# Transformer block stack: residual stream kept tokens-on-partitions, softmax mask added by VectorE, maximum subtracted by GpSimd, P.V two slots later

## What is computed

```
for i in range(6):
    # attention: x @ Wqkv, 16 heads of 64; q and k normalised by head, rotated (rotary tables with scale)
    # windows of 32 queries, 64 keys; sim = 8 q.k, masked, softmax, times v
    x = attn_layer(shift_tokens(x), Wqkv[i], ...) + x            # ends in out @ Wo
    # layernorm over 128 channels, W1 to 2 x 341, a * gelu(gate), W2, with biases
    x = ffn_layer(shift_tokens(x), ln_g[i], ln_b[i], W1[i], b1[i], W2[i], b2[i]) + x
def shift_tokens(t):                                             # second half of the channels comes from the token before
    a, s = jnp.split(t, 2, -1)
    return jnp.concatenate([a, pad(s)[:, :-1]], -1)
```

## Time and profile before

| | us |
|---|---|
| median of three runs | 1746.93 (1746.7 to 1748.54) |
| the profiled execution, its own time | 1748.49 |
| its span, first to last instruction | 1746.7 |
| PE busy in the span | 1695.2 (97%) |
| VectorE (DVE) | 1391.6 (80%) |
| ScalarE (ACT) | 1232.3 (71%) |
| GpSimd (POOL) | 1129.3 (65%) |
| DMA queue of SyncE (q1) | 82512 packets, 116.84 MB, 27.8% of 16 engines |

### The profile page before, as it was taken

How to read it: one execution, slowest core, us unless ns; L and a number is a source line. 1 busy time by engine, 2 the same in 40 slices (tenths; PEclk the granted TensorE clock), 3 DMA queues, 4 the chain that set the end, 5 groups by cost and what they waited for, 6 DMA issues and landing times.

```text
span 1746.7 us, 72189 instructions
## 1 busy us (share of the span) xinstructions
PE 1695.2 (97%) x30558; PEld 1198.8 (69%) x30558; DVE 1391.6 (80%) x2607; ACT 1232.3 (71%) x2173; POOL 1129.3 (65%) x1066
## 2 busy tenths in 40 slices
PE   5889999999999999999999999999999999999996
PEld 2356777777777777777777777777777777777774
DVE  4688888888888888888888888888888888888762
ACT  2256777777777677777777777777777777777763
POOL 0477676667766766776676676667766666776640
PEclk9799999999999999999999999999999999999998
DMA  3133223323222332222323322322322332322222
GB/s 106 24 93 69 61 57 75 84 70 71 66 59 73 86 75 59 71 61 61 89 66 80 71 60 60 86 70 71 77 63 56 75 88 70 71 63 59 59 56 73
DMA packets 82830, 121.45 MB, mean 70 GB/s; under 512 B 25168, under 2 KB 28752, under 8 KB 82256
## 3 DMA queue, kind: packets, MB, share of 16 engines
q1 hardware_dynamic: 82512, 116.84, 27.8%
HBM read 20.28 MB, written 2.10 MB: 13 GB/s over the span
## 4 chain that ended last, share of the span: by engine, by line
PE 94%; DVE 3%; ACT 2%; issue 1%; DMA 0%; SPq 0%; POOL 0%; DVEq 0%; POOLq 0%; ACTq 0%
PE QKb L452 20%; PE O L543 12%; PE F L525 11%; PE S L452 9%; PE VTb L475 9%; PE S L501 9%; PE S L513 5%; PE F L598 4%; PE F L553 4%; PE F L599 3%; PE S L494 2%; PE F L568 2%; PE F L587 1%; DVE t L833 1%; PE F L560 1%
## 5 line engine op out<-in xcount | busy, mean ns | idle before, releaser
L833 DVE TENSOR_TENSOR t<-QKb,table 128x1024 f32<-128x1024 f32 x384 | 469.3, 1222 | 191.2 <-ACT sq L648 190.9
L977 POOL TENSOR_TENSOR t<-t 128x512 f32<-128x512 f32 x384 | 488.1, 1271 | 202.1 <-DVE t L833 201.1
L956 POOL TENSOR_TENSOR t<-t,rn 128x512 f32<-128x512 f32 x384 | 401.0, 1045 | 163.7 <-DVE rn L880 163.7
L648 ACT ACTIVATE sq<-QKb 128x512 f32<-128x512 f32 x384 | 229.3, 597 | 377.6 <-PE QKb L452 377.6
L452 PE MATMUL QKb<-wq_sb,x_sh 128*128 128x512 f32 x768 | 412.4, 619 | 11.2 <-DVE t L833 10.6
L475 PEld LDWEIGHTS VTb<-cst,t 128*128 128x128 f32 x1536 | 191.9, 141 | 200.2 <-issue 199.0
L842 DVE TENSOR_REDUCE ss<-sq 128x16 f32<-128x1024 f32 x192 | 232.0, 1208 | 0.0
L475 PE MATMUL VTb<-cst,t 128*128 128x128 f32 x1536 | 230.7, 273 | 0.0
L543 PEld LDWEIGHTS O<-PT,V 64*64 64x64 f32 x12288 | 196.7, 135 | 48.2 <-issue 42.4
L543 PE MATMUL O<-PT,V 64*64 64x32 f32 x12288 | 218.0, 221 | 0.4 <-DVE rn L880 0.4
L963 POOL TENSOR_TENSOR E<-E,rs 128x512 f32<-128x512 f32 x192 | 200.0, 1042 | 14.8 <-DVE rs L889 14.7
(11 more groups left out here) (137 smaller groups left out, 2464.2 us busy)
## 6 DMA issues: line engine op xcount, KB each, us to landing
V<-v_tok SPq DMA_DIRECT2D x1440, 64.0 KB, 2.0
wq_sb<-in_wqkv SPq DMA_DIRECT2D x36, 256.0 KB, 3.0
wo_sb<-in_wo SPq DMA_DIRECT2D x6, 512.0 KB, 4.3
w_sb<-in_w SPq DMA_DIRECT2D x6, 341.0 KB, 3.3
w_sb<-in_w SPq DMA_DIRECT2D x6, 192.0 KB, 3.0
y_spill<-OT SPq DMA_DIRECT2D x1, 1024.0 KB, 4.2
V<-y_spill SPq DMA_DIRECT2D x1, 1024.0 KB, 8.3
out<-V SPq DMA_DIRECT2D x4, 256.0 KB, 2.9
```

The costliest lines, as they stand in the source:

```text
L648: act.activation(sq[:, v % 4, :], QK_ps, ACT.Square).then_inc(sq_done, 1)
L833: dve.tensor_tensor(t12[:, v, :, :].rearrange("p c (h d) -> p c h d", h=8), QK_ps.rearrange("p (h d) -> p h d", h=8).unsqueeze(1) .to_broa ...
L956: pool.tensor_tensor(w, w, rn[:, vv // 4, 8 * (vv % 4):8 * (vv % 4 + 1)].unsqueeze(2) .to_broadcast([P, 8, DH]), ALU.mult).then_inc(qk_nor ...
L977: pool.tensor_tensor(w, w, t12[:, v, 1, :].rearrange("p (h c d) -> p h c d", h=8, c=2)[:, :, ::-1, :], ALU.add).then_inc(add_done, 1)
```

## The change

**Softmax.** The two mask products on PE go. VectorE adds the mask (float32, from the constants) to the scores as it reads them from PSUM into `E`, then takes the maximum from `E`. GpSimd subtracts it in place (new lag `L_SUB` = 12). Exp moves from lag 12 to 13, the product with the reciprocal from 13 to 14, PT from 14 to 16, PV from 16 to 18, Wo from 20 to 22.

**Residual stream.** `xt` holds tokens on the partitions. Wo and W2 exchange their operands, so the activations are the stationary side and each product is cut into two of 128 columns. The shifted copy `xs` is made by three DMAs of SyncE (after `mid_done`, but written at lag `F_SH` = 24, ahead of the V moves of that slot). The layernorm is `bn_stats` and `bn_aggr` on VectorE (`F_ST` = 28), then an add, a power and two `tensor_scalar` on GpSimd (`F_NM` = 28), and two transposes on PE (`F_XT` = 29) that ScalarE reads with gain and bias (`F_AFF` = 29). The next step's input needs two transposes more (`TX` = slot 6), and ScalarE stages `x_sh` from PSUM. b2 is a row of W2, beside a constant row of `hid`.

**Ends.** No transposes after the last product: y is loaded earlier and transposed by PE in the drain (`Y_BACK`), silu, product and sum go by batch, and the output in 8 stores. The scan uses two PSUM banks instead of three.

```
-L_S, L_EXP, L_NORM, L_PT, L_PV = 11, 12, 13, 14, 16
-F_WO, F_MID, F_MEAN, F_CENT, F_SQ, F_VAR, F_VCOPY, F_DIAG = 20, 25, 26, 27, 27, 27, 28, 27
-F_BC, F_XN, F_AFF, F_W1, F_GEL, F_HID, F_W2, F_END = 28, 30, 31, 33, 33, 34, 35, 36
+L_S, L_SUB, L_EXP, L_NORM, L_PT, L_PV = 11, 12, 13, 14, 16, 18
+F_WO, F_MID, F_SH, F_ST, F_NM, F_XT, F_AFF = 22, 26, 24, 28, 28, 29, 29
+F_W1, F_GEL, F_HID, F_W2, F_END = 34, 34, 35, 36, 36
+TX = 6
...
+                    f, pr = batch(s, par, v, F_SH)
+                    if f is not None:
+                        wait(sp, mid_done, f + 1)
+                        wait(sp, normed, f * NT)
+                        sp.dma_start(xs[:, :, 0:D // 2], xm[:, pr, :, 0:D // 2]).then_inc(xs_moved, 16)
+                        sp.dma_start(xs[1:P, :, D // 2:D], xm[0:P - 1, pr, :, D // 2:D]).then_inc(xs_moved, 16)
+                        sp.dma_start(xs[0:1, 1:NT, D // 2:D], xm[P - 1:P, pr, 0:NT - 1, D // 2:D]).then_inc(xs_moved, 16)
...
-                        for p in range(2):
-                            pe.matmul(S2[:, p, 0:4 * KEYS], ident_bf[:, :], mask_bf[:, :], start=True, stop=False,
-                                      skip_group_check=True)
...
+                    f, pr = batch(s, par, v, F_XT)
+                    if f is not None:
+                        wait(pe, normed, (f + 1) * NT)
+                        wait(pe, ff_final, f)
+                        wait(pe, x_staged, staged(s, v))
+                        for t in range(NT):
+                            mm = pe.transpose(BANK_XT[:, P * t:P * (t + 1)], xn[:, t, :], ident)
+                        mm.then_inc(xnT_ready, 1)
...
-                                mm = pe.matmul(BANK_WO[:, 0:N], wo_sb[:, h, :], OT[:, pr, h, :],
-                                               start=(h == 0), stop=(h == HP - 1))
+                                for t in range(NT):
+                                    mm = pe.matmul(BANK_WO[:, D * t:D * (t + 1)], OT[:, pr, h, P * t:P * (t + 1)],
+                                                   wo_sb[:, h, :], start=(h == 0 and t == 0), stop=(h == HP - 1),
+                                                   skip_group_check=True)
...
-                        wait(pe, mid_done, upto(f + 2, STEPS))
+                        wait(pe, mid_done, begun(s, v, F_WO))
...
+                    if v == TX and live(s + 1, STEPS):
+                        wait(pe, ff_final, s + 2 - B)
+                        wait(pe, ff_final, begun(s, v, F_W2))
+                        wait(pe, xn_done, begun(s, v, F_XT))
+                        for t in range(NT):
+                            mm = pe.transpose(BANK_TX[:, P * t:P * (t + 1)], xt[:, (s + 1) % B, t, :], ident)
+                        mm.then_inc(tx_ready, 1)
...
+                        dve.tensor_tensor(Ek, Sv, cst[:, C_MASK:C_MASK + 4 * KEYS]
+                                          .rearrange("p (c k) -> p c k", k=KEYS).unsqueeze(1)
+                                          .to_broadcast([P, 2, 4, KEYS]), ALU.add).then_inc(mask_done, 1)
+                        wait(dve, mask_done, a + 1)
+                        wait(dve, sub_done, a - 3)
+                        dve.tensor_reduce(mx[:, k, :], E[:, k, :].rearrange("p (c k) -> p c k", k=KEYS), AX_X, ALU.max)\
+                           .then_inc(max_done, 1)
...
+                        for t in range(NT):
+                            dve.bn_stats(ln6[:, t, :], xs[:, t, :]).then_inc(ln6_done, 1)
+                        wait(dve, normed, f * NT)
+                        for t in range(NT):
+                            wait(dve, ln6_done, f * NT + t + 1)
+                            dve.bn_aggr(ln2[:, t, :], ln6[:, t, :]).then_inc(ln2_done, 1)
...
+                        pool.tensor_tensor(w, w, mx[:, k, :].unsqueeze(2).to_broadcast([P, 8, KEYS]),
+                                           ALU.subtract).then_inc(sub_done, 1)
...
+                        pool.tensor_tensor(rstd[:, :], ln2[:, :, 1], eps2[:, :], ALU.add).then_inc(rstd_done, 1)
+                        wait(pool, rstd_done, 2 * f + 1)
+                        pool.tensor_tensor(rstd[:, :], rstd[:, :], minus_half[:, :], ALU.pow).then_inc(rstd_done, 1)
+                        wait(pool, rstd_done, 2 * f + 2)
+                        wait(pool, xnT_ready, f)
+                        for t in range(NT):
+                            pool.tensor_scalar(xn[:, t, :], xs[:, t, :], ln2[:, t, 0:1], rstd[:, t:t + 1], ALU.subtract, ALU.mult)\
+                                .then_inc(normed, 1)
```

More of the change, by code:

```diff
@@ L55 @@
 C_ALL = C_TAB + 4 * NT * DH
[L57 to L58 removed]
+R_G, R_B, R_B1A, R_B1G = 0, 1, 2, 2 + NCH
+R_ALL = 2 + 2 * NCH
 def live(unit, count):
@@ L381, in _ @@
             all_steps(sp, step)
+            sp.wait_ge(y_saved, 16)
             sp.wait_ge(o_ready, QUADS)
+            sp.dma_start(y_back, y_spill).then_inc(in_y, 16)
             sp.dma_start(x_tok, x.rearrange("b (t p) d -> p (b t) d", p=P)).then_inc(in_x2, 16)
[L385 to L391, removed]
+            for b in range(B):
+                sp.wait_ge(o_done, b + 1)
+                sp.dma_start(out[b].rearrange("(t p) d -> p t d", p=P), o_tok[:, NT * b:NT * (b + 1), :])\
+                  .then_inc(stored, 16)
+            sp.wait_ge(stored, 16 * B)
         @block.tensor
@@ L468, in step @@
                     recurrence(in_fill(s, v, 0))
+                    u, vv, st, pr = unit(s, par, v, L_V)
+                    if live(u, UNITS) and vv % 2 == 0:
+                        c = vv // 2
+                        if vv < 4 and pr == 0:
+                            wait(pe, in_v[c], 16 * (st // B + 1))
+                        wait(pe, v_evac, v_units(st, vv, 0) - 1)
+                        wait(pe, mask_done, s_units(s, v))
+                        project(V_ps, pr, c // 2, V_COLS[c % 2]).then_inc(v_ready, 1)
                     u, vv, st, pr = unit(s, par, v, L_TR)
@@ L547, in step @@
                         mm.then_inc(o_ready, 1)
+                    if s * SLOTS + v == Y_BACK:
+                        wait(pe, in_y, 16)
+                        wait(pe, pt_evac, QUADS)
+                        wait(pe, v_evac, STEPS * (SLOTS // 2))
+                        wait(pe, o_evac, QUADS)
+                        for t in range(TILES):
+                            mm = pe.transpose(banks[t // 4][:, P * (t % 4):P * (t % 4 + 1)],
+                                              y_back[:, t // NT, P * (t % NT):P * (t % NT + 1)], ident)
+                        mm.then_inc(yT_ready, 1)
                     f, pr = batch(s, par, v, F_W2)
@@ L708, in step @@
                         gelus(f, pr, [0, 1])
+                    if v == TX and live(s + 1, STEPS):
+                        wait(act, tx_ready, s + 1)
+                        wait(act, qk_ready, s * SLOTS)
+                        wait(act, v_ready, s * (SLOTS // 2))
+                        stage(BANK_TX[:, 0:N], 1 - par)
             def gelus(f, par, chunks):
@@ L837, in step @@
                                           ALU.mult).then_inc(t12_done, 1)
+                    f, pr = batch(s, par, v, F_END)
+                    if f is not None:
+                        finish(f, pr)
+                    a, k, st, pr = quad(s, par, v, L_S)
+                    if live(a, QUADS):
+                        wait(dve, s_ready, a + 1)
+                        Sv = S2[:, :, 0:4 * KEYS].rearrange("p b (c k) -> p b c k", k=KEYS)
+                        Ek = E[:, k, :].rearrange("p (c b k) -> p b c k", c=4, b=2)
+                        wait(dve, pt_ready, a - 3)
+                        if a == 0:
+                            wait(dve, yT_done, 4)
+                        dve.tensor_tensor(Ek, Sv, cst[:, C_MASK:C_MASK + 4 * KEYS]
[5 more added lines that the diff above has]
+                           .then_inc(max_done, 1)
                     u, vv, st, pr = unit(s, par, v, L_SS)
```

278 lines of the change are left out of this document (99 added, 179 removed).

## The result

The changed kernel takes 1807.93 us (median of 4 runs, 1801.84 to 1810.02), against 1747.05 before: ratio 1.034, 95% interval 1.0323 to 1.0357. That is 66 us above the forecast and outside its range.

What follows compares the result with a forecast made beforehand. PE was taken to bound the 34.15 us step. From the profiled 1748.5: - 32 (steps) + 24.5 (changes of layer) + 2 (V columns) + 0.5 (ends) = 1743.5, as median 1742 us; 8-in-10 range 1719 to 1770.

Steps and rivals of the forecast that it cites:

- PE's work and the half products: PE's step: 2.08 us removed, 0.44 added, 34.15 to 32.5; Wo and W2 in half products cost nothing extra.
- Weight loads: Rival in Wo and W2: 44 loads of 0.085 us show before their products, 1912 us; chance 0.03.
- The odd slots and the walk: Slot-by-slot walk of PE and VectorE: waits of 0.58, 0.10 and 0.27 us, step 33.5, gain 0.68 a step, 32 in all.
- The wait for `xm` before W1: Slot 2: VectorE adds the residual only after slot 1's work, so W1 waits for `mid_done`, 0.27 us a step.
- the second of my rivals: All of PE's saved work shows because VectorE's slots run evenly: 1697 us, or 1671 with the first rival; chance 0.04.
- the loop: Loop through QKb: next QK waits for the rotation, so a slot takes at least 3.07 us; binds in slot 5.
- GpSimd hidden: GpSimd's subtractions and normalisation raise it from 23.7 to 28.7 us a step, 86% of 33.5, late nowhere in the walk.
- Where the DMAs bite: the change of layer: SyncE's queue delays `prm`; ScalarE stands 5.5 us, 4.9 lost per change of layer, 24.5 in five; V columns 2 more.
- The V columns: Reloaded at lag 11, they land about 0.4 us late in slot 6 at each change of layer: 2 us in all.
- The ends: Start saves 0.5 us in casts; drain about even; +1 taken in all, bounds -5 and +5, +0.5 in the sum.
- SyncE's queue: Rival at layer changes: each 0.1 us more per issue costs 11 us, 1764 at 0.85; chance 0.29 including a further wait.
- the first rival: The weights come in time at layer changes: `prm` 1 us late, 5 x 1 instead of 24.5 and 2, 1721 us; chance 0.20.

Runs made afterwards that it cites:

- shift_in_16: Changed kernel with the shifted copy's 127-row transfer cut into 112 and 15 rows, one issue more: 1787.58 us, 1.024 of the kernel before.
- v_loads_on_act: Changed kernel with only the reload of the V columns issued by ScalarE instead of SyncE: 1771.01 us, 1.0138 of the kernel before.

## Why the prediction was wrong, by its own steps

- **PE's work and the half products: right.** Four half products (`L552`, eight records) take 0.89 us in the chain, two whole ones (four records) took 0.86; what I counted as 22 and 44 products are records. Weight loads don't show.
- **The odd slots and the walk: right in its main wait.** 33.33 to 33.35 us a step for 33.5, the wait of PE for `t` 72 times and 37.0 us in all. The wait for `xm` before W1 (0.27 in the walk) didn't come: the trace has one, of 0.7 us, in the whole run. In its place P.V waits for Newton in slot 2 (0.16 of idle, and 1.13 to 1.22 for 1.06), and that the sum of the step fits so well is in part luck. Taking slot 5's shortage away brought the step to 32.6, near the 32.5 of PE's work alone; this also says that the second of my rivals (all of PE's work shows) needs only another place for Wo, where I had written that the loop forbids it.
- **GpSimd hidden: right, though one bound was wrong.** It is busy for 28.65 us of a step, as forecast (28.7), but a `tensor_scalar` on 128 elements takes 0.795 us, where my bound was 0.4; the subtractions, at 1.04, were as taken. With the measured durations my own sum gives 29.1, so the match to 0.1 is luck.
- **"Where the DMAs bite: the change of layer": wrong, and it decided the sign.** The mechanism and the place were right (the reloads come late because the shifted copy and 22 V moves stand before them), and this term of the sum was mis-sized: 26.5 us forecast, 92 measured by the step lengths, 89 by the run without reloads. ScalarE waited 9.9 us for `prm` each time, forecast 5.5. Three things were short in it.
  - *The queue.* From the residual sum's end to the issue of the V columns' load it took 15.15 us (880.65 to 895.80), forecast 11.5. The third issue is 2.2 of the 3.65, the V moves 1.0 (15 in 10.8, two of them over 1 us), the first two issues 0.4. With "0.6 or less each" I had bounded the three issues by the earlier trace rows, where no transfer comes from 127 rows. Without the hold, and with the extra issue that this needs, the 39 steps are 16 us shorter (`shift_in_16`).
  - *The V columns* were to be 0.4 us late. With 3.65 more it is 4 (4.6 measured; the tables below make up most of the difference), and the step with them is 7.9 us longer than an ordinary one, 0.5 of it the tables': where my sum had a term of 2 us these are 37, by step lengths and by `v_loads_on_act` alike. I had put the queue's rival at 2.2 us of loss for each 0.1 us of an issue, at one path per change of layer; there are two, three steps apart, and each pays the full delay.
  - *PE's clock.* After each of the ten holes PE's products run at the lower level for about 5 us. From the chain, V, TR, PT and Wo after the V columns' landing take 1.21 + 0.41 + 0.41 + 0.50 = 2.5 us more than in an ordinary step. Ten times 2.5 is an estimate of 25 us that stood nowhere in my sum.
- **Left out: the scale tables.** Their two products on VectorE (1.85 us, `L790` in the chain) now stand before a rotation, but most of that time fits in: the run without reloads, which still computes them, has 33.8 us in that step for 33.3. That is 0.5 a layer, some 2.5 us in all.
- **The ends: short of what I had.** Outside the 39 steps the profiled executions took 415.5 us after and 414.1 before. I had counted 46.5 steps of steady work; by that count another seven steps should be 0.8 shorter there, so start and drain lost about 7 us (an estimate), where I had +0.5 and a bound of +5. The chain of the drain shows most of it: the shifted copy stands in it twice, 4.87 and 4.77 us to land behind its issues, where ScalarE had copied before.
- **The rival "SyncE's queue"** named the place and the sign, and its example even the 254 short pieces; its price (1764) was too low by the same three things. What it took for the cause, the shortness of the pieces alone, is refuted; it is that 127 rows put them on one engine.
- **Slips that change nothing.** "1671 with the first rival" should be 1676, since that rival keeps 5 x 1 us; 0.69 a move gives 1746.4, not over 1746.9; 44 loads of 0.085 over 46.5 steps are 174, not 170.

Added up, a change of layer of 18.4 us is 7.4 for the V columns, 0.5 for the tables, 8.4 in the step in which `prm` is late and 2.1 in the step behind it. That last part is the lower clock again: in the chain from 1014.04 on, QK, TR, S and Wo take 2.07, 0.85, 1.11 and 2.00 us, where an ordinary step has 0.90, 0.44, 0.79 and 1.09. The two parts affect each other: the V columns and the FFN's weights are worth 37 and 41 us singly and 73 together. How long PE must stand before its clock falls was not tried.

## What to carry to other kernels

Before work is put ahead of a weight load in a queue, add up the queue from the event that its first instruction waits for to the load's issue, for every load in it, and compare with the slack; a load with 2 us to spare doesn't survive 15 issues. Ask on how many DMA engines a transfer runs: one from 127 rows is slow itself and holds all behind it, and cutting it into 112 and 15 costs one more issue, 0.9 us here. Look also at the drain, where nothing hides a copy's landing. And where the profile puts a wait down to a DMA, see which instruction ends at a fixed distance before the wait does. Where the profile shows PE idle for several microseconds, count the products behind the hole at the lower clock too.

## What the hardware showed that I had not expected

- A transfer from 127 partitions moves at 18 GB/s with 0.09 of the DMA engines busy, one from 128 at 82; the issue behind it is held for 2.7 us (0.59 for a V move, 0.76 behind the unshifted half), 0.92 behind 112 rows, and 0.93 behind 127 rows in 512-byte pieces, which are half as many.
- After each of the ten holes, in which PE had stood for 4.2 to 7.9 us, its granted clock was 0.50 to 0.65 for 4 to 5 us, and 1.00 again from 904.6 on in the first one shown; over the whole span it was 0.967, and 0.991 before.
- GpSimd's `tensor_scalar` with two values per partition costs 0.795 us for 128 elements, three quarters of a `tensor_tensor` on 512 (1.04).
